# Attention on blocks of eight heads by four keys: mixing on 64x32 tiles, turned keys' blocks on VectorE, halves added on GpSimd

## What is computed

```python
q, k, v = qkv[0], qkv[1], qkv[2]            # 8 heads of 8 features
qgr, _ = jnp.linalg.qr(q)
kgr, _ = jnp.linalg.qr(k)
attn_grass = jnp.einsum('bhnd,bhmd->bhnm', qgr, kgr) ** 2 * grassman_scale
dots = jnp.einsum('bhnd,bhmd->bhnm', q, k)
attn_eucl = dots * scale
attn_riem = dots ** 2 * riem_scale
a = jnp.concatenate([attn_eucl, attn_riem, attn_grass], axis=1)   # 24 channels
a = (a - bn_mean) * inv + bn_beta
a = jnp.einsum('oc,bcnm->bonm', conv_w, a) + conv_b               # mixes 24 into 8
a = jax.nn.softmax(a, axis=-1)
out = jnp.einsum('bhnm,bhmd->bhnd', a, v)
```

## Time and profile before

| | us |
|---|---|
| median of 3 runs (1018.27 to 1019.19) | 1018.49 |
| the profiled execution | 1019.19 |
| its span in the profile | 1017.5 |
| TensorE busy | 898.6 (88%) |
| VectorE busy | 763.6 (75%) |
| GpSimd busy | 488.2 (48%) |
| ScalarE busy | 423.6 (42%) |
| mean granted TensorE clock | 0.944 |

### The profile page before, as it was taken

One profiled execution on the slowest core, in us unless ns is written; L12 is line 12 of the kernel. 1 busy time (PEld: TensorE's weight loads), 2 busy tenths in 40 slices (PEclk: granted clock), 3 DMA queues, 4 the chain that ended last, 5 costly groups with the idle time before them and its releaser, 6 DMA issues. The chain is left out here.

```text
span 1017.5 us, 37672 instructions
## 1 busy us (share of the span) xinstructions
PE 898.6 (88%) x15018; PEld 577.8 (57%) x15018; DVE 763.6 (75%) x1287; ACT 423.6 (42%) x710; POOL 488.2 (48%) x551
## 2 busy tenths in 40 slices
PE   3677668998937999999999999999999999799995
PEld 2233245555525666666666666666666666446663
DVE  4588863887983888888788888888888888747773
ACT  2333423112713444444444444444444444257774
POOL 3355631110007666666666666666666666212220
PEclk9777877998977999999999999999999999979998
DMA  8765000324102111111111111111111111001111
GB/s 300 263 223 202 1 0 1 55 54 115 31 0 64 50 49 50 52 52 52 48 45 48 50 52 52 52 49 46 48 49 50 52 52 53 2 3 29 29 29 32
DMA packets 64446, 63.25 MB, mean 62 GB/s; under 512 B 37081, under 2 KB 55068, under 8 KB 64412
## 3 DMA queue, kind: packets, MB, share of 16 engines
q1 hardware_dynamic: 63884, 61.25, 20.4%
q10 hardware_dynamic: 528, 1.54, 0.4%
HBM read 52.93 MB, written 6.75 MB: 59 GB/s over the span
## 5 line engine op out<-in xcount | busy, mean ns | idle before, releaser
L1163 ACT ACTIVATE sq<-ps_dot 128x752 f32<-128x752 f32 x192 | 153.1, 798 | 302.6 <-PE ps_dot L1042 302.6
L1042 PE MATMUL ps_dot<-q_st,k_blk 32*64 32x94 f32 x6144 | 169.4, 247 | 3.1 <-POOL k_blk L1002 3.1
L1042 PEld LDWEIGHTS ps_dot<-q_st,k_blk 32*64 32x64 f32 x6144 | 134.4, 133 | 64.6 <-issue 50.0
L1002 POOL TENSOR_TENSOR k_blk<-k_turn,hmask 128x384 f32<-128x384 f32 x64 | 65.3, 1020 | 177.8 <-ACT k_turn L1151 177.8
L1210 DVE TENSOR_REDUCE sums<-prob 128x94 f32<-128x564 f32 x128 | 148.0, 1201 | 2.0 <-ACT prob L1156 2.0
L1006 POOL TENSOR_TENSOR k_mix<-k_cm,cols 128x768 f32<-128x768 f32 x64 | 119.8, 1872 | 0.0
L988 POOL TENSOR_TENSOR v_blk<-v_rep,vmask 128x384 f32<-128x384 f32 x128 | 106.6, 854 | 6.8 <-PE ps_m L1074 6.8
L1091 PEld LDWEIGHTS ps_a<-q_st,k_mix 64*64 64x64 f32 x3072 | 77.1, 132 | 56.4 <-issue 48.2
L1091 PE MATMUL ps_a<-q_st,k_mix 64*64 64x94 f32 x3072 | 101.0, 250 | 0.8 <-DVE prob L1198 0.8
L1156 ACT ACTIVATE prob<-prob,cols 128x564 f32<-128x564 f32 x128 | 91.1, 758 | 20.4 <-DVE prob L1198 20.4
L1181 DVE TENSOR_REDUCE row_max<-ps_a 128x94 f32<-128x564 f32 x128 | 89.3, 741 | 12.4 <-PE ps_a L1110 12.4
(11 more groups left out here) (225 smaller groups left out, 1389.7 us busy)
## 6 DMA issues: line engine op xcount, KB each, us to landing
v_rep<-v_rows SPq DMA_DIRECT2D x256, 96.0 KB
x_g<-in_x_dram SPq DMA_DIRECT2D x15, 1500.0 KB, 6.7
v_rows<-tok SPq DMA_DIRECT2D x32, 96.0 KB
q_st<-q_cm SPq DMA_DIRECT2D x64, 47.0 KB
out_dram<-rows SPq DMA_DIRECT2D x16, 188.0 KB
x_g<-in_x_dram ACTq DMA_DIRECT2D x1, 1500.0 KB, 7.4
top_rows<-tok SPq DMA_DIRECT2D x16, 32.0 KB
top<-top_rows SPq DMA_DIRECT2D x1, 512.0 KB, 3.4
```

Of the source, the lines that this page charges most:

```text
L1002: return pool.tensor_tensor(k_blk[:, a, :, kind], view.unsqueeze(2).broadcast_to([128, NTAU, 4, 8]), k["hmask4"][:].unsqueeze(1).unsqueeze ...
L1042: mm = pe.matmul(ps_dot[64 * hg:64 * hg + 64, (a + g) % 2, b, col:col + N], k_blk[rows, a, 2 * (2 * g + t2) + mi].rearrange("p k h m -> p ...
L1163: act.activation(sq[:, :, :, 2 * g:2 * g + 2, :].rearrange("p mi b t n -> p b mi (t n)"), ps_dot[:, (a + g) % 2, :, 0:4 * N].rearrange("p ...
```

## The change

What one block of weights holds is laid out differently. Before, a block of 32 rows holds four heads by eight keys; after, a block of 64 rows holds all eight heads by four keys, with the keys of a block next to each other. What follows from that:

- `dots`: 16 matmuls a group as before, now on 64x64 tiles; the batch b picks the rows and the bank, the kind v (plain or turned) picks the columns. ps_dot has three banks and the squares are taken in six instructions instead of three.
- `mixing`: all 24 linear matmuls first (`linear`), then 16 matmuls of 282 columns on 64x32 tiles (`squares_mixed`), four for each of b and v; the logits take four banks.
- The turned keys' blocks are built by VectorE straight from PSUM (`key_blocks`), placed after the row maxima and before the maximum per head. ScalarE's copy, and the loop over it, go. Turning moves from behind the third dots to behind the first.
- VectorE's sums of exponentials go. GpSimd adds the first three groups of keys to the last three (`halves`), and TensorE adds the rest up: 6 matmuls a pair for the denominators instead of 2.
- Subtraction and exponentials are issued per batch; the padded keys are masked through a bias of the exponential instead of a constant in the subtraction. The exponentials of the first batch stand before the last two squares.
- `attended` and `denominators` move ahead of the third dots.
- The programs of TensorE and SyncE are written out for all pairs; those of ScalarE, VectorE and GpSimd keep their loops.
- Constants: two permutation matrices more, other small columns. The values are stored and loaded in plain order, two transfers a pair instead of four; the keys are written out in an order by blocks.

```diff
@@ queries_keys (orthogonalise)
-                    act.activation(out[:, span(c, CP), :], ps_turn[:, 4 + 2 * a + s, 0:CP * NP].rearrange("p (r m) -> p r m", r=CP),
-                                   ACT.Identity, bias=k["qkv_bias"][:, s:s + 1]).then_inc(qk_out, 1)
+                    dst, src = out[:, span(c, CP), :], ps_turn[:, 4 + 2 * a + s, 0:CP * NP]
+                    if s == 0:
+                        src = src.rearrange("p (r m) -> p r m", r=CP)
+                    else:
+                        dst, src = dst.rearrange("p r (t x) -> p r x t", t=NT), src.rearrange("p (r x t) -> p r x t", r=CP, t=NT)
+                    act.activation(dst, src, ACT.Identity, bias=k["qkv_bias"][:, s:s + 1]).then_inc(qk_out, 1)
@@ attend, GpSimd
+            def halves(j, a):
+                pool.wait_ge(s["exp_done"], 2 * j + 2)
+                if later(j, 1):
+                    pool.wait_ge(s["av_done"], j)
+                pool.tensor_tensor(half[:], prob[:, a, :, 0:3, :], prob[:, a, :, 3:6, :], ALU.add).then_inc(s["half_done"], 1)
+
+            def build(i, a, n, has_next):
+                if later(i, 3):
+                    halves(i - 3, 1 - a)
                 if later(i, 2):
-                    pool.wait_ge(s["keys_used"], i - 1)
...
+                    pool.wait_ge(s["keyed"], 2 * (i - 1))
+                pool.tensor_tensor(k_blk[:, a, :, 0], k_cm[:, span(i, 1), :].rearrange("p i (u m) -> p (i u) m", m=4).unsqueeze(2).broadcast_to([128, NT * SLOTS, H, 4]),
+                                   k["hmask"][:].unsqueeze(1).unsqueeze(3).broadcast_to([128, NT * SLOTS, H, 4]), ALU.mult).then_inc(s["keys_ready"], 1)
+                pool.tensor_tensor(k_mix[:, a].rearrange("p t x o -> p (t x) o"), k_cm[:, span(i, 1), :].rearrange("p i m -> p (i m)").unsqueeze(2).broadcast_to([128, NP, H]),
+                                   k["conv1"].unsqueeze(1).broadcast_to([128, NP, H]), ALU.mult).then_inc(s["mix_ready"], 1)
+                if has_next:
+                    turning(i + 1, 1 - a)
                 if later(i, 1):
                     values(i - 1, 1 - a, n)
@@ attend, TensorE
+                for c in range(SLOTS):
+                    for v in range(2):
                         for b in range(2):
+                            rows = slice(64 * b, 64 * b + 64)
+                            mm = pe.matmul(ps_dot[64 * v:64 * v + 64, (2 * g + b) % 3, N * c:N * c + N],
+                                           k_blk[rows, a, SLOTS * (3 * v + g) + c].rearrange("p k h m -> p (k h m)"), q_st[rows, a, :], start=True, stop=True)
                 mm.then_inc(s["dots_done"], 1)
...
+            def squares_mixed(i, b, v):
+                for c in range(SLOTS):
+                    mm = pe.matmul(ps_a[32 * c:32 * c + 32, 2 * b + v, 0:3 * N], k["mix_w"][64 * v:64 * v + 64, :],
+                                   sq[64 * v:64 * v + 64, b, c].rearrange("p t n -> p (t n)"), start=False, stop=True, skip_group_check=True)
                 return mm
...
+            def mixing(i):
+                pe.wait_ge(s["squared"], 6 * i + 5)
+                squares_mixed(i, 0, 0)
+                pe.wait_ge(s["keyed"], 2 * i + 1)
+                squares_mixed(i, 0, 1).then_inc(s["mixed"], 1)
+                pe.wait_ge(s["squared"], 6 * i + 6)
+                squares_mixed(i, 1, 1)
+                pe.wait_ge(s["keyed"], 2 * i + 2)
+                squares_mixed(i, 1, 0).then_inc(s["mixed"], 1)
+
+            def step(i, a):
                 dots(i, a, 0)
+                if i + 1 < PAIRS:
+                    turn_keys(i + 1, 1 - a)
+                if i >= 1:
                     turn_max(i - 1)
                 dots(i, a, 1)
+                if i >= 1:
                     spread_max(i - 1)
+                if i >= 2:
+                    attended(i - 2, a)
+                    denominators(i - 2)
                 dots(i, a, 2)
+                linear(i, a)
+                mixing(i)
@@ attend, ScalarE
             def step(i, a, has_prev, has_prev2, has_next):
+                squares(i, 0)
+                squares(i, 1)
+                if has_prev:
+                    exps(i - 1, 1 - a, 0)
+                squares(i, 2)
+                if has_prev:
+                    exps(i - 1, 1 - a, 1)
@@ attend, VectorE
+            def key_blocks(i, a):
+                dve.wait_ge(s["kt_done"], i + 1)
+                dve.tensor_tensor(k_blk[:, a, :, 1], ps_m[:, KT_AT:KT_AT + NP].rearrange("p (u m) -> p u m", m=4).unsqueeze(2).broadcast_to([128, NT * SLOTS, H, 4]),
+                                  k["hmask"][:].unsqueeze(1).unsqueeze(3).broadcast_to([128, NT * SLOTS, H, 4]), ALU.mult).then_inc(s["turned_ready"], 1)
...
             def step(i, a, has_prev, has_prev2, has_next):
                 if has_prev:
                     maxima(i - 1)
+                if has_next:
+                    key_blocks(i + 1, 1 - a)
+                if has_prev:
+                    heads_max(i - 1)
                     shifted(i - 1, 1 - a)
-                    if has_prev2:
-                        output(i - 2)
-                    sums_of(i - 1, 1 - a)
-
+                if has_prev2:
+                    output(i - 2)
```

More of the change, by code:

```diff
@@ L639, in _ @@
             for a in range(2):
[L640 removed]
+                sp.wait_ge(stored[a], 32 * NCH // 2)
         @block.tensor
@@ L970, in load @@
                 for b in range(2):
[L971 to L979 removed]
+                    src = v_dram[span(2 * i + b, 1)].rearrange("b (x t) f -> x (b t f)", t=NT)
+                    sp.dma_start(v_rep[:, a, b, :], src.unsqueeze(1).broadcast_to([16, H, NT * C])).then_inc(v_in[a], 16)
+            for i in range(PAIRS):
+                load(i, i % 2)
         @block.gpsimd
@@ L1010, in build @@
                 if later(i, 1):
                     values(i - 1, 1 - a, n)
-            build(0, 0, 0)
-            build(1, 1, 1)
-            with pool.Fori(1, PAIRS // 2) as twice:
-                build(2 * twice, 0, twice)
-                build(2 * twice + 1, 1, twice + 1)
+            turning(0, 0)
+            for i in range(4):
+                build(i, i % 2, (i + 1) // 2, True)
+            with pool.Fori(2, PAIRS // 2 - 1) as twice:
+                build(2 * twice, 0, twice, True)
+                build(2 * twice + 1, 1, twice + 1, True)
@@ L1066, in attended @@
                         pe.matmul(ps_m[64 * b:64 * b + 64, AV_AT:AV_AT + N], v_blk[:, a, b, t, :], prob[:, a, b, t, :],
-                                  start=(t == 0), stop=(t == NT - 1))
[L1069 to L1072, removed]
-                for b in range(2):
-                    mm = pe.matmul(ps_m[64 * b:64 * b + 64, DEN_AT:DEN_AT + N], k["den_w"][:], sums[:, b, :], start=True, stop=True)
-                mm.then_inc(s["av_done"], 1)
@@ L1119, in step @@
-            def step(i, a, has_prev, has_prev2, has_next):
+                for t in range(NT):
+                    for b in range(2):
+                        for w in range(2):
+                            half_of = slice(64 * w, 64 * w + 64)
+                            mm = pe.matmul(ps_a[half_of, 2 * b + t // 3, N * (t % 3):N * (t % 3) + N],
+                                           k_mix[64 * b:64 * b + 64, a, t, 8 * w:8 * w + 8].rearrange("p x o -> p (x o)"), q_st[64 * b:64 * b + 64, a, :],
+                                           start=(t % 3 == 0), stop=False, skip_group_check=True)
+                        if t == NT - 1:
+                            mm.then_inc(s["keyed"], 1)
@@ L1129, in step @@
-                if has_prev2:
-                    attended(i - 2, a, False)
-                    denominators(i - 2, i)
-                else:
-                    logits_free(i)
-                mixing(i, a)
+                linear(i, a)
+                mixing(i)
             turn_keys(0, 0)
-            steps(pe, step)
+            for i in range(PAIRS):
+                step(i, i % 2)
             turn_max(PAIRS - 1)
             spread_max(PAIRS - 1)
-            attended(PAIRS - 2, 0, False)
```

248 lines of the change are left out of this document (99 added, 149 removed).

## The result

The changed kernel takes 1094.85 us in the median of 4 runs (1092.81 to 1098.67), the kernel before 1018.47 in 4 runs beside it. The ratio is 1.0753, with a 95% interval of 1.0721 to 1.0785. The prediction was 968 us, with a range of 946 to 1014: a gain was forecast, and it is a loss. The profiled execution of the changed kernel has a span of 1092.0 us and a mean granted clock of 0.888; before they were 1017.5 us and 0.944.

What follows compares the result with a forecast made beforehand. TensorE bounds the kernel, with VectorE nearly as late. A pair of 8.10 for 8.87 us saves 48.5 over 63 intervals; with 1.9-0.5 from the edges, 50 us, giving 968 us from the median, range 946 to 1014.

Steps and rivals of the forecast that it cites:

- copies (0.36): VectorE's copies of the heads' maximum, on TensorE's path after the key blocks: 0.36 us, ending at 3.07.
- walk of the new pair: Timeline of one attention pair from the first dots at 0 to the end at 8.10 us, for 8.87 before.
- part (5): GpSimd's work per pair: together 6.7 to 7.4 us, under the pair's 8.1, hence hidden, with 0.7 us of cover.
- what would show it: Signs to check: mixing about 1.2 us, spread waiting 0.8, pair 8.1, GpSimd waiting once a pair, clock 1.00.
- rival (b): TensorE's stall lowers the clock; one spell per pair gives 1075 us. Most pairs, or written-out code too slow: 0.07; some spells: 0.06.
- wait ahead of the spread: TensorE, done with the second dots at 2.3 us, waits 0.8 us for VectorE's key blocks, heads' maximum and copies.
- mixing, start to next dots: TensorE's 16 matmuls on 64x32 tiles, row halves side by side: 1.24 us for 2.51, bounds 1.05 and 2.0.
- first dots of the stage earlier: At the stage's start, the first dots wait behind only 1.9 us of GpSimd blocks: 1.9 us gained.
- Rival (a): The mixing's row halves don't overlap on TensorE: mixing 1.97 us, pair 8.83, about 1015 us; chance 0.11.
- Rival (c): VectorE's key blocks take 1.1 us for 0.96, plus small waits: pair 8.3, 982 us; inside the forecast's 0.64.
- (d): Written-out code, 64 steps for 6, not supplied in time: 1 us per pair gives 1031; 0.07 shared with the falling clock.
- The case "slower": The whole kernel gets slower instead of faster: chance 0.09, against 0.88 for faster and 0.03 for the same.

Runs made afterwards that it cites:

- copy_from_psum: Changed kernel with the heads' maximum written to PSUM and VectorE's two copies reading it there; 965.07 us, ratio 0.9474.
- gpsimd_waits: Changed kernel, copies still from SBUF, with GpSimd starting k_mix only after VectorE's copies, its loop written out; 957.92 us, ratio 0.9409.
- blocks_later: Changed kernel with VectorE's blocks of turned keys moved behind the heads' maximum and the copies; 1099.45 us, ratio 1.0784.
- stall_filled: Changed kernel with six matmuls nobody reads run on TensorE ahead of the spread, copies still from SBUF; 1037.21 us, ratio 1.0179.

## Why the prediction was wrong

**The step that failed** is "copies (0.36)" in the walk of the new pair, with "It is hidden" of GpSimd in part (5) as its other half. The 0.36 us came from the earlier trace rows, and that row is right for its own neighbourhood: it was read without the GpSimd rows of the same microsecond, in which GpSimd is idle. The walk then moved the copies 0.7 us later (2.71 us after the first dots, for 2.03 in the earlier trace rows) and doubled GpSimd's own blocks ahead of k_mix, and never asked what the two engines would do at the same time. It took "hidden" to be a question of GpSimd's sum (6.7 to 7.4 us in 8.1). The sum was if anything too high: the groups measured 1.51, 1.51, 0.41, 1.18 and 2 x 0.855, together 6.3 us. GpSimd waits in every pair, as asked for under "what would show it". What mattered was when, not how much. What the runs showed in its place: the two copies take 1.67 us instead of 0.36, because each ends only with the GpSimd instruction in flight, and TensorE waits 1.97 us instead of 0.8.

The Trainium skill has the rule, and the prediction did not weigh it. "SBUF — State Buffer", Who interferes with whom, says that a VectorE copy which uses both its ports, and an operation with two SBUF inputs against a GpSimd instruction that reads SBUF, share a port pair with GpSimd; whoever starts first keeps it for the whole instruction, and one with at most one SBUF input outside the fast modes is free. The traces agree with each: 219 ns became 861 for the copy (94x128, 86 of them from 400 to 840 us) and 926 for two inputs, while the key blocks, with one input in PSUM, took 958 beside GpSimd's own blocks, as forecast from their elements. That this copy uses both ports no trace shows directly.

**Then the size of the stall.** With 1.97 us for 0.8, the mechanism of rival (b) came true, in two of three pairs. The prediction argued against it that "this stall is 0.8 and not 1.14 us": for 0.8 that was right (copy_from_psum: clock 1.00 with a wait of 0.81 in each pair). Rival (b)'s 1075 was nearest of all cases, but that is luck, as its price was made up otherwise: 1.7 us of doubled streaming in each pair. Measured are 58 us for the clock, two spells of 1.4 and 1.55 us (10.66 and 10.81 less 9.26) in three pairs, and 72 us for the stall, for which it had nothing beyond the forecast's.

**The terms that held,** by copy_from_psum and the trace of after:

| step | forecast | measured |
|---|---|---|
| pair, with the copies free | 8.10 us | 8.085 |
| wait ahead of the spread | 0.8 | 0.81 |
| mixing, start to next dots | 1.24 | 1.21 |
| key blocks on VectorE, 768 elements | 0.96 | 0.958 |
| heads' maximum | 0.42 | 0.41 |
| squares on ScalarE, 376 elements | 0.48 | 0.482 |
| four exponentials on ScalarE | 1.9 | 2.10 (2 x 0.609 and 2 x 0.442) |
| sum of halves on GpSimd, 564 elements | 1.17 to 1.4 | 1.181 |
| linear blocks k_mix on GpSimd | 1.87 | 1.51 |
| first dots of the stage earlier | 1.9 | 1.9 (8.55 us behind L905's start at 300.79 before, 6.66 behind L916's at 300.51) |
| whole kernel | 968 | 965.07 |

k_mix is off most: the same 768 elements in another order (the eight heads last instead of in the middle), the keys read one after the other and not in steps of 12; which of the two counts no run tells. The exponentials cost 0.2 us more, on an engine with time to spare; by the rate of the squares, which the text names, they would have been 1.6. The 568 us of the attention stage are 64 times 8.87, where the stage runs some 582 (305 to 887); no later sum uses them. Rival (a) falls by the mixing's 1.21 us. Rival (c) falls by the blocks' 0.958. Of (d), nothing shows: from the fourth on every pair of copy_from_psum takes 8.08 to 8.35 us, though TensorE's pairs are all written out. The agreement of 968 with 965 doesn't excuse the number, as the kernel that was to be predicted has its copies in SBUF, and it is in part luck: copy_from_psum pays 0.13 us a pair for slower copies, which the forecast didn't have. Its true counterpart is gpsimd_waits, with the copies at 0.36 us as forecast. There the wait is 0.68 us for 0.8, the pair 7.95 for 8.10 and the time 958 for 968, so the walk was 0.15 us a pair too long.

**What the range lacked.** The case "slower" had 0.09, and its rivals were searched for on TensorE (tiles, clock, code) and in the length of the key blocks. The side that failed is one where two engines off the bound meet on a resource that neither's busy time shows.

## What to carry to other kernels

Before work is added or moved on GpSimd, list the VectorE instructions on the path whose operands all lie in SBUF, and read GpSimd's rows of the same microseconds; a duration taken from a stretch where GpSimd is idle is no price for one where it isn't. If they meet, let the VectorE instruction read one operand from PSUM (282 ns for 219 here), or make GpSimd wait for it (free here, where GpSimd had the time). And price a stall twice, for itself and for the clock: here a stall of 1.97 us a pair instead of 0.81 cost 72 us for itself and 58 by the clock, while 0.81 us a pair cost no clock.

## What the runs showed of the hardware

- **A VectorE copy from SBUF to SBUF waits for the end of the GpSimd instruction in flight**, and ends 0.08 us behind it. Of two copies in a row, the second waits for the next GpSimd instruction as well: that one starts ahead of it (604.15 in blocks_later, 610.60 in after). The pair of copies costs 1.67 us in after, 1.96 in blocks_later, and 0.36 with GpSimd idle.
- **Nothing in the busy times tells of it.** A held copy is shown as busy, not as waiting, so VectorE looked merely slower at this line. The sign is a mean far above that of the same form elsewhere (861 for 219 ns), with a minimum and maximum wide apart (439 and 1304).
- **Eight tiles of 64x32 stream together:** 32 records of 282 columns in 1.28 us, where one group after another would take 1.9. With the row halves grouped less well it is 1.46, as the second row of passes starts 0.31 us behind the first instead of 0.12.
- **The same stall of 1.99 us brought the clock down in two of three pairs**, in a rhythm that breaks once between 400 and 840 us. Why it spares the third is open. A wait of 0.81 us in each pair (copy_from_psum), or of 0.48 idle behind the useless matmuls (stall_filled), never did so between 400 and 800 us.
